# A fused transformer kernel: the masks of a top-16 attention move from VectorE to GpSimd for five of eight tiles

## The chip, the cores and the metric

One NeuronCore of one Trainium2 chip. The time is that of one execution on the device in microseconds (us); lower is better. Engines in the profile: PE is TensorE (PEld its weight loads), DVE is VectorE, ACT is ScalarE, POOL is GpSimd, SP is SyncE.

## The reference, cut to what matters

The program runs four blocks (L0 to L3) on x of shape (2, 1024, 256). The change is in the last, L3, between its cross-attention that keeps the 16 largest of 64 scores in each head, and its gated MLP:

```python
TOPK, H, D, HID = 16, 16, 16, 1024

def _topk_cross_attn(h, ctx, ...):
    q = (h @ w_q + b_q).reshape(B, L, H, D)
    kv = (ctx @ w_kv + b_kv).reshape(B, Lc, 2, H, D)       # Lc = 64
    scores = einsum('bqhd,bkhd->bhqk', q, k) / sqrt(D)
    top_s, top_i = jax.lax.top_k(scores, TOPK)
    attn = jax.nn.softmax(top_s, axis=-1)
    o = (attn weighted sum of the 16 rows of v that top_i names)
    return o @ w_co + b_co

def _swiglu(h, ...):
    u = h @ w_m1 + b_m1
    a, b = (u[..., :HID], u[..., HID:])
    return jax.nn.silu(a) * b @ w_m2 + b_m2

h = _ln(x) * (1 + sc_mca) + sh_mca
h = _topk_cross_attn(h, context, ...)
x = x + h * g_mca
h = _ln(x) * (1 + sc_mlp) + sh_mlp
x = x + _swiglu(h, ...) * g_mlp
```

## The kernel before, in words

Each engine has its own program, written out by hand; semaphores tie them together. A loop of two iterations runs over the batch (1024 tokens each), and inside it the blocks follow one another. The 1024 tokens of a batch are T = 8 tiles of 128 tokens (one token in each partition), and NB = 2 blocks of TB = 4 tiles. In the top-16 stage a tile is a matrix of 128 x 1024 scores: 16 heads of 64 context positions.

A tile t goes through these steps; the functions carry these names in the code:

- PE `top_scores(t)` (L1143) writes the scores to PSUM, ACT `top_copy(t)` (L1602) copies them into `prob3`, a ring of three buffers ("prob" in the profile).
- DVE `best(t)` (L2193) takes the 8 largest of each head into `m8` ("m" in the profile), 16 instructions MAX8, one for each head. DVE `mark(t)` (L2198) writes a copy of the scores into `taken`, where those 8 are replaced by LOWEST (16 pairs of MATCH_VALUE_LOAD and MATCH_REPLACE8). DVE `next_best(t)` (L2205) and `mark_next(t)` (L2210) do the same once more on `taken`. What equals LOWEST in `taken` then is the top 16. `taken` and `m8` have two buffers each.
- POOL `centre(t)` (L2405) subtracts each head's maximum from `prob3` as soon as `mark(t)` is done; ACT `exp(t)` (L1606) exponentiates it.
- DVE `mask(t)` (L2216) multiplies the exponentials by (taken == LOWEST), in one instruction, SCALAR_TENSOR_TENSOR.
- PE `top_turn(t)` (L1158) transposes the result, in two halves, ACT `turned(t)` (L1613) copies it into `probT`, PE `top_values(t)` (L1165) multiplies by the values and the ones that give the sums.
- DVE `divide(t)` (L1845, L1848) divides by the sums; PE `top_turn_outputs(t)` (L1172) turns the output, ACT `outputs3(t)` (L1617) copies it into `oT`.

Between these, PE runs matmuls on a constant tile (`keep_busy`, L565) that compute nothing which is used.

After four tiles the first block's output goes through the projection `wco` (PE L448), is turned (L589) and added to x on DVE (`add(0, 6)`: L1812 and the statistics L1795 to L1800); POOL's `ln(7, (0,))` (L2292) makes the reciprocal deviation, DVE `normalise(7, 0)` (L1805) the normalised tokens, PE turns them (L457), and ACT writes them twice (L1290): `hT` in full and `hs` rounded. The difference between the two, `hTlo`, is made by POOL's `tokens3_lo(0)` (L2410). Then the MLP of block 0 begins, while tiles 5 to 7 are still in the top-16 stage: PE `up(n)` (L1188), ACT `hidden(n)` (L1629 and L1290) reads it, POOL `times(n)` (L2416) multiplies the two halves, ACT `product_hi(n)` (L1640) rounds the product, POOL `product_lo(n)` (L2421) takes the rest, PE `down(n)` (L1217) uses both. For n < 5 the last three are POOL's, for later n they are DVE's.

Every engine works strictly in the order that is written, so a wait holds back all that stands behind it on that engine. The lines that set DVE's order are in the loop over t at the end of the stage; for POOL they are the plain list of calls behind `centre(0)`.

## Time and profile before

| | |
|---|---|
| three runs | 1786.18, 1791.75, 1791.81 us |
| median | 1791.75 us |
| the profiled execution: its own time | 1789.12 us |
| its span, first to last instruction | 1787.0 us |
| mean granted TensorE clock over the span | 0.951 |
| busy: PE, PEld | 1575.8 us (88%), 917.6 us |
| busy: DVE, ACT, POOL | 1082.2 us (61%), 812.6 us (45%), 417.7 us (23%) |
| the top-16 stage, first `best` to last `divide` | 750.46 to 867.90 us and 1604.48 to 1720.69 us |

The profile gives for each instruction its start and length on its engine, and, in square brackets, how long the engine sat idle before it and which instruction released it. The stage occurs twice, once for each batch, about 854 us apart. The granted clock is given as a share of full speed, where 1.00 is 2.4 GHz and 0.50 is 1.2 GHz.

### The profile page before, as it was taken

To read this page: it belongs to the slowest core of one execution; us is meant where nothing else is said; L and a number is where in the kernel's file an instruction comes from. 1 tells how busy PE (TensorE), PEld (TensorE's weight loads), DVE (VectorE), ACT (ScalarE), POOL (GpSimd) and SP (SyncE) were. 2 spreads that over 40 slices of the span, in tenths; PEclk is the share of its full clock that TensorE was granted. 3 is DMA by queue.
4 is the path that set the end of the run, shared out by engine and by line. 5 is a ranking of instruction groups with operands and counts; after the bars stand their busy time and mean duration, and the time that the engine had idled before them with its cause. 6 is when DMAs were issued, how large, how long until landed. Compare 5 with 4: busy or idle time off the path is not lost.

```text
span 1787.0 us, 27133 instructions
## 1 busy us (share of the span) xinstructions
PE 1575.8 (88%) x9541; PEld 917.6 (51%) x9541; DVE 1082.2 (61%) x2933; ACT 812.6 (45%) x1283; POOL 417.7 (23%) x418
## 2 busy tenths in 40 slices
PE   3789998999988989877878899899998888987888
PEld 1536564434343756455653556543443365654566
DVE  1464243899726338799536433479991643879963
ACT  1134331388843535324533434138886353442454
POOL 0140003433006024113205000153300602412230
PEclk8799999999999999999998999999999999999899
DMA  9200004422010000000050000352201000000004
GB/s 318 95 1 1 0 1 135 61 38 38 2 71 1 1 1 2 1 1 1 1 166 2 1 1 1 111 84 38 38 2 72 1 1 1 2 1 1 1 1 141
DMA packets 43332, 64.02 MB, mean 36 GB/s; under 512 B 8634, under 2 KB 32061, under 8 KB 42301
## 3 DMA queue, kind: packets, MB, share of 16 engines
q1 hardware_dynamic: 32845, 40.73, 6.9%
q0 software_dynamic: 8448, 14.96, 5.6%
q10 hardware_dynamic: 1904, 6.55, 0.9%
q8 instruction: 81, 1.33, 0.3%
q14 instruction: 54, 0.44, 0.1%
HBM read 47.28 MB, written 2.10 MB: 28 GB/s over the span
## 4 chain that ended last, share of the span: by engine, by line
PE 38%; issue 37%; POOL 12%; DVE 8%; ACT 3%; SPq 2%; DMA 1%; POOLq 0%; ACTq 0%; DVEq 0%
PE ps L932 7%; PE ps L944 7%; PE ps L1188 4%; PE ps L448 3%; POOL wkblk L2396 3%; PE ps L1022 3%; PE ps L917 3%; PE ps L1030 2%; PE ps L565 2%; PE ps L1217 2%; DVE taken L2198 2%; DVE taken L2210 1%; POOL rstd L2292 1%; DVE m L2193 1%; PE ps L457 1%
## 5 line engine op out<-in xcount | busy, mean ns | idle before, releaser
L2067 DVE TENSOR_REDUCE mm<-ps 128x1 f32<-128x1024 f32 x256 | 309.6, 1223 | 36.7 <-PE ps L917 30.0
L1490 ACT ACTIVATE pt<-ps 128x512 f32<-128x512 f32 x512 | 276.9, 598 | 62.8 <-PE ps L932 53.6
L2292 POOL TENSOR_TENSOR rstd<-ve,minus_half 128x4 f32<-128x4 f32 x32 | 36.2, 1130 | 810.7 <-DVE ve L1800 810.7
L932 PE MATMUL ps<-qx,kx 64*128 64x512 f32 x512 | 192.0, 452 | 1.8 <-ACT pt L1490 1.0
L917 PE MATMUL ps<-kx,qx 48*128 48x512 f32 x512 | 189.5, 450 | 1.7 <-DVE mm L2067 1.7
L944 PE MATMUL ps<-pt,v 128*32 128x256 f32 x2048 | 161.2, 396 | 0.0
L932 PEld LDWEIGHTS ps<-qx,kx 64*128 64x128 f32 x512 | 80.0, 186 | 98.2 <-ACT pt L1490 92.9
L1956 DVE TENSOR_TENSOR rlo<-ring,rhi 128x512 fp32r<-128x512 f32 x48 | 33.2, 692 | 127.7 <-ACT ring L1441 127.6
L917 PEld LDWEIGHTS ps<-kx,qx 48*128 48x128 f32 x512 | 76.6, 187 | 25.8 <-issue 15.4
L944 PEld LDWEIGHTS ps<-pt,v 128*32 128x32 f32 x2048 | 43.3, 109 | 87.8 <-ACT pt L1490 63.7
L457 PE MATMUL ps<-ident,xhat 128*128 128x128 f32 x288 | 45.0, 309 | 44.9 <-DVE xhat L1805 43.2
L565 PE MATMUL ps<-filler 128*128 128x512 f32 x258 | 81.8, 439 | 0.2
L2334 POOL DMA_DIRECT2D qx<-mxT x64 | 31.8, 506 | 211.2 <-ACT mxT L1482 190.8
L2396 POOL TENSOR_TENSOR wkblk<-kT,head_mask 128x1024 f32<-128x1024 f32 x32 | 60.5, 1896 | 85.3 <-PE ps L1085 82.2
L1812 DVE TENSOR_TENSOR x<-x,ps 128x1024 f32<-128x1024 f32 x32 | 39.0, 1218 | 67.6 <-PE ps L589 67.5
L1441 ACT ACTIVATE rhi<-ps,mod 128x512 fp32r<-128x512 f32 x48 | 33.1, 689 | 102.2 <-PE ps L722 102.2
L1290 ACT ACTIVATE hT<-ps,mod 128x512 f32<-128x512 f32 x48 | 35.1, 775 | 86.4 <-PE ps L457 86.4
L457 PEld LDWEIGHTS ps<-ident,xhat 128*128 128x128 f32 x288 | 38.1, 159 | 59.7 <-DVE xhat L1805 52.0
L1581 ACT ACTIVATE wprobT<-ps 128x1024 f32<-128x1024 f32 x32 | 32.8, 1023 | 75.1 <-PE ps L1097 75.1
L1859 DVE TENSOR_REDUCE mxw<-ps 128x16 f32<-128x1024 f32 x32 | 37.7, 1219 | 48.1 <-PE ps L606 48.1
L1085 PE MATMUL ps<-wkblk,qT 128*128 128x512 f32 x128 | 60.0, 594 | 1.5 <-DVE v L2140 1.5
L1805 DVE TENSOR_SCALAR xhat<-x,mv,rstd 128x256 f32<-128x256 f32 x128 | 46.3, 424 | 21.4 <-POOL rstd L2292 20.9
(322 smaller groups left out, 3454.0 us busy)
## 6 DMA issues: line engine op xcount, KB each, us to landing
w<-in_L_xcond_e_w_dram SPq DMA_DIRECT2D x9, 512.0 KB, 8.0
w<-in_L_xcond_e_w_dram SPq DMA_DIRECT2D x3, 1536.0 KB, 12.1
wm<-in_L_xcond_W_mlp_dram SPq DMA_DIRECT2D x4, 1024.0 KB, 7.9
qx<-q_hi POOLq DMA_DIRECT2D x64, 64.0 KB, 2.6
kx<-k_hi POOLq DMA_DIRECT2D x64, 64.0 KB, 2.8
w3a<-in_L_xcond_w_m_dram SPq DMA_DIRECT2D x2, 2048.0 KB, 8.1
s_ada<-in_L_xcond_w_ada_dram ACTq DMA_DIRECT2D x1, 2304.0 KB, 14.7
qx<-q_lo POOLq DMA_DIRECT2D x32, 64.0 KB, 2.6
```

The costliest lines, as they stand in the source:

```text
L448: ins = pe.matmul(ps[:, bank, :], w[:, c, m * P:(m + 1) * P], src[:, c, :], start=c == 0, stop=c == KC - 1)
L457: ins = pe.transpose(ps[:, bank + c, t * P:(t + 1) * P], src[:, TB * k + t, c * P:(c + 1) * P], ident[:, :])
L565: pe.matmul(ps[:, bank, :], filler[:, 0:P], filler[:, :], start=True, stop=True)
L917: ins = pe.matmul(ps[:, bank + half, :], qx[r, p % 4, t * P:(t + 1) * P], kx[r, p % 4, half * 512:(half + 1) * 512], start=True, stop=True)
L932: pe.matmul(ps[:, bank, :], kx[r, p % 4, kc * P:(kc + 1) * P], qx[r, p % 4, half * 512:(half + 1) * 512], start=True, stop=True).then_inc( ...
L944: ins = pe.matmul(ps[o:o + 32, 7, q:q + BLK // 2], v2[:, kc, VS * (2 * p + e):VS * (2 * p + e) + 32], pt[:, (2 * kc + e) % 8, half * BLK + ...
L1085: ins = pe.matmul(ps[:, 2 * (u % 2) + half, :], qT[:, t // TB, c, t % TB * P:(t % TB + 1) * P], wkblk[:, u % 2, 4 * half:4 * half + 4, :]. ...
L1188: ins = pe.matmul(ps[:, 4 + i, :], w3ap[wp][:, c, (NC_HID * i + m) * P:(NC_HID * i + m + 1) * P], src[:, c, :], start=(wp, part, c) == (0, ...
L1490: act.activation(pt[:, u % 8, half * 512:(half + 1) * 512], ps[:, bank, :], ACT.Exp, scale=QK_SCALE).then_inc(st_read, 1)
L2067: return dve.tensor_reduce(mm[:, p % 2, e, t:t + 1], place(), X, ALU.max).then_inc(ring_read, 1)
L2292: pool.tensor_tensor(rstd[:, k, :], ve[:, k, :], minus_half[:, :], ALU.pow).then_inc(rstd_ready, 1)
L2396: pool.tensor_tensor(wkblk[:, u % 2, :, :], kT3[:, t // TB, c, t % TB * P:(t % TB + 1) * P].unsqueeze(1).broadcast_to([P, HC, P]), head_ma ...
```

## The change

- A constant `N_PMASK = 5`. For tiles 0 to 4 the mask is no longer DVE's. POOL's new `mask(t)` waits for `mark_next(t)` (semaphore `top_taken`), turns `taken` in place into ones and zeros (TENSOR_SCALAR is_equal, 128x1024), and, once `exp(t)` is done, multiplies `prob3` by it (TENSOR_TENSOR, 128x1024). Tiles 5 to 7 keep DVE's mask.
- `top_ready` becomes two semaphores, one for each engine that masks; PE's `top_turn(t)` waits for the one of its tile. DVE's `best(t)` for t = 2 to 6 waits in addition until POOL has masked tile t - 2, whose buffers it will overwrite.
- DVE's `divide(t - 1)` comes behind `mark_next(t)` for t = 1, 2 and 3 (before: ahead of it) and between `next_best(t)` and `mark_next(t)` for t = 4 to 7. `add(0, 6)` of tile 5 comes behind `mark(5)`, `normalise(7, 0)` behind `next_best(5)` and ahead of the division.
- `tokens3_lo(0)` is DVE's, behind `mark_next(5)` and ahead of `mask(5)`; before, it was POOL's.
- POOL's `centre(5)` comes ahead of `ln(7, (0,))`, and `centre(6)` ahead of `product_lo(0)` and `times(1)`.
- ACT's `product_hi(0)` comes ahead of `hidden(1)`.
- `keep_busy` between the tiles 0 to 3 has 3 and 8 matmuls where it had 4 and 10.

```diff
--- before.py
+++ after.py
@@ -81,6 +81,7 @@
 N_CU = NB * KC
 N_POOL3 = 5
 N_DVE3 = NB * NC_HID - N_POOL3
+N_PMASK = 5


 def key_entries(p):
@@ -291,8 +292,8 @@
...
-        ts_ready, ts_read, top_marked, top_sub, top_exp, top_ready, tp_turned, tpT_ready, tpv_done, to_ready, to_turned, toT_ready = (sem(n) for n in (
...
+        ts_ready, ts_read, top_marked, top_sub, top_exp, tp_turned, tpT_ready, tpv_done, to_ready, to_turned, toT_ready = (sem(n) for n in (
...
@@ -308,6 +309,7 @@
         h2_done, h2_ready, w22_done = sem("h2_done"), sem("h2_ready"), sem("w22_done")
         h3_done, h3_read, w32_done = sem("h3_done"), sem("h3_read"), sem("w32_done")
         w3_hi, w3_split, hs3_hi, hs3_lo, h3_hi = sem("w3_hi"), sem("w3_split"), sem("hs3_hi"), [sem("hs3_lo0"), sem("hs3_lo1")], sem("h3_hi")
+        top_taken, top_flag, top_ready = sem("top_taken"), sem("top_flag"), [sem("top_ready_pool"), sem("top_ready_dve")]
         prod_pool, prod_dve, lo_pool, lo_dve = sem("prod_pool"), sem("prod_dve"), sem("lo_pool"), sem("lo_dve")
         v_done, v_ready, v2_clear = sem("v_done"), sem("v_ready"), sem("v2_clear")
         ring_ready, ring_read, hi_ready, lo_ready, full_done, full_ready = (sem(n) for n in (
@@ -1146,7 +1148,10 @@

                 def top_turn(t):

-                    pe.wait_ge(top_ready, t0 + t + 1)
+                    if t < N_PMASK:
+                        pe.wait_ge(top_ready[0], b * N_PMASK + t + 1)
+                    else:
+                        pe.wait_ge(top_ready[1], b * (T - N_PMASK) + t + 1 - N_PMASK)
                     if t == 0:
                         pe.wait_ge(qT_ready, b * 2 * N_Q + 6)
                     else:
@@ -1227,10 +1232,10 @@
                 top_scores(1)
                 for t in range(TB):
                     top_scores(t + 2)
-                    keep_busy(5, 4)
+                    keep_busy(5, 3)
                     if t:
                         top_turn_outputs(t - 1)
-                    keep_busy(5, 10)
+                    keep_busy(5, 8)
                     top_turn(t)
                     top_values(t)
                 keep_busy(5, 4)
@@ -1668,8 +1673,8 @@
                 ln(7, 0, (mod, M3_SC_ML, M3_SH_ML), 6)
                 hidden(0)
                 turned(5)
+                product_hi(0)
                 hidden(1)
-                product_hi(0)
                 exp(6)
                 product_hi(1)
                 hidden(2)
@@ -2188,6 +2193,8 @@

                 def best(t):
                     dve.wait_ge(ts_read, t0 + t + 1)
+                    if 2 <= t < N_PMASK + 2:
+                        dve.wait_ge(top_ready[0], b * N_PMASK + t - 1)
                     dve.sem_inc(passed, 1)
                     for h in range(H):
                         ins = dve.max(m8[:, t % 2, h, 0:8], scores_by_head(t)[:, h, :])
@@ -2208,12 +2215,15 @@
                 def mark_next(t):
                     for h in range(H):
                         ins = dve.match_replace(taken_by_head(t)[:, h, :], m8[:, t % 2, h, 8:16], taken_by_head(t)[:, h, :], LOWEST)
-                    link(ins)
+                    if t < N_PMASK:
+                        ins.then_inc(top_taken, 1)
+                    else:
+                        link(ins)

                 def mask(t):

                     dve.wait_ge(top_exp, t0 + t + 1)
-                    dve.scalar_tensor_tensor(prob3[:, t % 3, :], taken[:, t % 2, :], LOWEST, prob3[:, t % 3, :], ALU.is_equal, ALU.mult).then_inc(top_ready, 1)
+                    dve.scalar_tensor_tensor(prob3[:, t % 3, :], taken[:, t % 2, :], LOWEST, prob3[:, t % 3, :], ALU.is_equal, ALU.mult).then_inc(top_ready[1], 1)

                 def divide(t):
                     outputs(t, 3, t0, tpv_done, to_turned, to_ready)
@@ -2244,18 +2254,21 @@

                 for t in range(T):
                     best(t)
+                    mark(t)
                     if t == TB + 1:
                         add(0, 6)
-                    mark(t)
-                    if t in (TB, TB + 1):
+                    next_best(t)
+                    if t == TB + 1:
+                        normalise(7, 0)
+                    if t >= TB:
+                        divide(t - 1)
+                    mark_next(t)
+                    if 1 <= t < TB:
                         divide(t - 1)
                     if t == TB + 1:
-                        normalise(7, 0)
-                    next_best(t)
-                    if t and t not in (TB, TB + 1):
-                        divide(t - 1)
-                    mark_next(t)
-                    mask(t)
+                        tokens3_lo(0)
+                    if t >= N_PMASK:
+                        mask(t)
                 divide(7)
                 times(5)
                 add(1, 2)
@@ -2404,10 +2417,14 @@
                     sc = prob3[:, t % 3, :].rearrange("p (h s) -> p h s", s=S)
                     pool.tensor_tensor(sc, sc, m8[:, t % 2, :, 0].unsqueeze(2).broadcast_to([P, H, S]), ALU.subtract).then_inc(top_sub, 1)

-                def tokens3_lo(k):
-
-                    pool.wait_ge(hs3_hi, b * NB + k + 1)
-                    pool.tensor_tensor(hTlo[:, k, :, :], hT[:, k, :, :], hs3[k][:, :, :].bitcast(F32), ALU.subtract).then_inc(hs3_lo[k], 1)
+                def mask(t):
+
+                    pool.wait_ge(top_taken, b * N_PMASK + t + 1)
+                    pool.sem_inc(passed, 1)
+                    pool.tensor_scalar(taken[:, t % 2, :], taken[:, t % 2, :], LOWEST, None, ALU.is_equal).then_inc(top_flag, 1)
+                    pool.wait_ge(top_flag, b * N_PMASK + t + 1)
+                    pool.wait_ge(top_exp, t0 + t + 1)
+                    pool.tensor_tensor(prob3[:, t % 3, :], prob3[:, t % 3, :], taken[:, t % 2, :], ALU.mult).then_inc(top_ready[0], 1)
                 n0 = b * NB * NC_HID

                 def times(n):
@@ -2424,15 +2441,16 @@
                 pool.wait_ge(v3_ready, b * NB + NB)
                 pool.sem_inc(passed, 1)
                 split3(2, w3b_hi[1][:, :, :], w3b_lo[:, NC_HID // 2:, :], w3b[:, NC_HID // 2:, :])
-                for t in range(1, 5):
+                mask(0)
+                for t in range(1, N_PMASK):
                     centre(t)
+                    mask(t)
+                centre(5)
                 ln(7, (0,))
-                centre(5)
-                tokens3_lo(0)
                 times(0)
+                centre(6)
                 product_lo(0)
                 times(1)
-                centre(6)
                 product_lo(1)
                 times(2)
                 product_lo(2)
```

How the order of the instructions moves. First DVE, the whole of tile 2, with the start of tile 3. In the rows m_151 is `m8` and prob_211 is `prob3`. Before:

```order
L2193 MAX m_151<-prob_211 128x8 x16
L2198 MATCH_REPLACE taken<-m_151,prob_211 128x64 x16
L2205 MAX m_151<-taken 128x8 x16
L1845 RECIPROCAL rs<-ps 128x16
L1848 TENSOR_TENSOR o_tok<-ps,rs 128x256
L2210 MATCH_REPLACE taken<-m_151,taken 128x64 x16
L2216 SCALAR_TENSOR_TENSOR prob_211<-taken,prob_211 128x1024
L2193 MAX m_151<-prob_211 128x8 x16
```

Now:

```order
L2200 MAX m_151<-prob_211 128x8 x16
L2205 MATCH_REPLACE taken<-m_151,prob_211 128x64 x16
L2212 MAX m_151<-taken 128x8 x16
L2217 MATCH_REPLACE taken<-m_151,taken 128x64 x16
L1850 RECIPROCAL rs<-ps 128x16
L1853 TENSOR_TENSOR o_tok<-ps,rs 128x256
L2197 REGISTER_ALU
L2200 MAX m_151<-prob_211 128x8 x16
```

The wide masking instruction is gone from the tile, and the division stands last in it. Second, DVE in tile 5, from `mark(5)` to the start of tile 6. Before:

```order
L2198 MATCH_REPLACE taken<-m_151,prob_211 128x64 x16
L1845 RECIPROCAL rs<-ps 128x16
L1848 TENSOR_TENSOR o_tok<-ps,rs 128x256
L1805 TENSOR_SCALAR xhat<-x,mv,rstd 128x256 x4
L2205 MAX m_151<-taken 128x8 x16
L2210 MATCH_REPLACE taken<-m_151,taken 128x64 x16
L2216 SCALAR_TENSOR_TENSOR prob_211<-taken,prob_211 128x1024
L2193 MAX m_151<-prob_211 128x8 x16
```

Now:

```order
L2212 MAX m_151<-taken 128x8 x16
L1810 TENSOR_SCALAR xhat<-x,mv,rstd 128x256 x4
L1850 RECIPROCAL rs<-ps 128x16
L1853 TENSOR_TENSOR o_tok<-ps,rs 128x256
L2217 MATCH_REPLACE taken<-m_151,taken 128x64 x16
L2237 TENSOR_TENSOR hTlo<-hT,hs_0_204 128x1024
L2226 SCALAR_TENSOR_TENSOR prob_211<-taken,prob_211 128x1024
L2197 REGISTER_ALU
L2200 MAX m_151<-prob_211 128x8 x16
```

`tokens3_lo(0)` (the write of hTlo) now stands on DVE between the search of tile 5 and its mask. Third, POOL from tile 4's centring to the MLP's second product. Before:

```order
L2405 TENSOR_TENSOR prob_211<-prob_211,m_151 128x1024
L2291 REGISTER_ALU
L2292 TENSOR_TENSOR rstd<-ve,minus_half 128x4
L2403 REGISTER_ALU
L2405 TENSOR_TENSOR prob_211<-prob_211,m_151 128x1024
L2410 TENSOR_TENSOR hTlo<-hT,hs_0_204 128x1024
L2416 TENSOR_TENSOR gate_0_195<-gate_0_195,up_0_197 128x512
L2421 TENSOR_TENSOR prod_lo_206<-gate_0_195,prod_hi_208 128x512
L2416 TENSOR_TENSOR gate_0_195<-gate_0_195,up_0_197 128x512
L2403 REGISTER_ALU
L2405 TENSOR_TENSOR prob_211<-prob_211,m_151 128x1024
```

Now:

```order
L2418 TENSOR_TENSOR prob_211<-prob_211,m_151 128x1024
L2422 REGISTER_ALU
L2424 TENSOR_SCALAR taken<-taken 128x1024
L2427 TENSOR_TENSOR prob_211<-prob_211,taken 128x1024
L2416 REGISTER_ALU
L2418 TENSOR_TENSOR prob_211<-prob_211,m_151 128x1024
L2304 REGISTER_ALU
L2305 TENSOR_TENSOR rstd<-ve,minus_half 128x4
L2433 TENSOR_TENSOR gate_0_195<-gate_0_195,up_0_197 128x512
L2416 REGISTER_ALU
L2418 TENSOR_TENSOR prob_211<-prob_211,m_151 128x1024
L2438 TENSOR_TENSOR prod_lo_206<-gate_0_195,prod_hi_208 128x512
```

POOL has two instructions more in each of the tiles 0 to 4, no hTlo, and centres tile 6 after one product instead of three instructions later.

## Rows read from the trace of the kernel before

**Rows 1.** The page's head and part 1: busy time and share of the span.
```profile
span 1787.0 us, 27133 instructions
PE 1575.8 (88%) x9541; PEld 917.6 (51%) x9541; DVE 1082.2 (61%) x2933; ACT 812.6 (45%) x1283; POOL 417.7 (23%) x418
```
**Rows 2.** The chain that ended last, 744 to 890 us: shares by line.
```profile
by line: issue 13.8%; DVE taken L2198 10.9%; DVE taken L2210 8.5%; PE ps L1188 7.3%; DVE m L2193 7.2%; PE ps L448 6.6%; DVE m L2205 5.7%; POOL gate L2416 5.1%; PE ps L1143 3.9%; POOL prob L2405 2.6%; POOL prod_lo L2421 2.6%; POOL hTlo L2410
```
**Rows 3.** Timeline, DVE, tile 1 of the first batch: start, length, line, operation.
```profile
763.49 2.12 DVE L2193 MAX8 m<-prob 128x8 f32<-128x64 f32 x16
...
771.15 0.26 DVE L1845 RECIPROCAL rs<-ps 128x16 f32<-128x16 f32 x1
...
775.01 1.22 DVE L2216 SCALAR_TENSOR_TENSOR prob<-taken,prob 128x1024 f32<-128x1024 f32 x1
776.15 2.12 DVE L2193 MAX8 m<-prob 128x8 f32<-128x64 f32 x16
```
**Rows 4.** Timeline, DVE, the mask of tile 0.
```profile
762.35 1.23 DVE L2216 SCALAR_TENSOR_TENSOR prob<-taken,prob 128x1024 f32<-128x1024 f32 x1 [1.01 <-ACT prob L1606]
```
**Rows 5.** Timeline, ACT and PE: exponential, transposes, values of tile 1.
```profile
772.68 1.05 ACT L1606 ACTIVATE prob<-prob 128x1024 f32<-128x1024 f32 x1
776.29 1.09 PE L1158 MATMUL ps<-ident,prob 128*128 128x128 f32 x8 [1.64 <-DVE prob L2216]
778.12 2.00 PE L1165 MATMUL ps<-vx,probT 128*128 128x64 f32 x16 [0.74 <-ACT probT L1613]
```
**Rows 6.** Groups of POOL by form: line, operation, count, busy us, mean ns, idle before.
```profile
L2405 POOL TENSOR_TENSOR prob<-prob,m 128x1024 f32<-128x1024 f32 x16 | 30.9, 1933 | 101.9 <-DVE taken L2198 101.9
...
L2372 POOL TENSOR_TENSOR w3b_lo<-w3b,w3b_hi 128x1024 fp32r<-128x1024 f32 x4 | 9.5, 2364 | 0.3
...
L2370 POOL CAST w3b_hi<-w3b 128x1024 fp32r<-128x1024 f32 x4 | 4.2, 1044 | 0.0
```
**Rows 7.** Timeline, DVE, from tile 5 on, first and then second batch.
```profile
814.11 2.12 DVE L2193 MAX8 m<-prob 128x8 f32<-128x64 f32 x16
...
823.41 2.35 DVE L1805 TENSOR_SCALAR xhat<-x,mv,rstd 128x256 f32<-128x256 f32 x4
...
831.07 1.23 DVE L2216 SCALAR_TENSOR_TENSOR prob<-taken,prob 128x1024 f32<-128x1024 f32 x1
832.21 0.98 DVE L2193 MAX8 m<-prob 128x8 f32<-128x64 f32 x7
...
847.79 2.12 DVE L2193 MAX8 m<-prob 128x8 f32<-128x64 f32 x16
...
882.17 1.38 DVE L1805 TENSOR_SCALAR xhat<-x,mv,rstd 128x256 f32<-128x256 f32 x4 [0.30 <-POOL rstd L2292]
...
1679.33 2.35 DVE L1805 TENSOR_SCALAR xhat<-x,mv,rstd 128x256 f32<-128x256 f32 x4
...
1689.12 2.11 DVE L2193 MAX8 m<-prob 128x8 f32<-128x64 f32 x16
...
1701.78 2.12 DVE L2193 MAX8 m<-prob 128x8 f32<-128x64 f32 x16
```
**Rows 8.** Timeline, ACT and POOL: rounded tokens hs, and hTlo, both batches.
```profile
1684.21 1.45 ACT L1290 ACTIVATE hs<-ps,mod 128x512 fp32r<-128x512 f32 x2
...
831.22 3.31 POOL L2410 TENSOR_TENSOR hTlo<-hT,hs 128x1024 fp32r<-128x1024 f32 x1 [6.57 <-ACT hs L1290]
...
1685.73 2.39 POOL L2410 TENSOR_TENSOR hTlo<-hT,hs 128x1024 fp32r<-128x1024 f32 x1 [5.17 <-ACT hs L1290]
```
**Rows 9.** Timeline, PE: transposes of tile 7, both batches.
```profile
862.76 1.07 PE L1158 MATMUL ps<-ident,prob 128*128 128x128 f32 x8 [0.43 <-ACT oT L1617]
...
1715.78 1.04 PE L1158 MATMUL ps<-ident,prob 128*128 128x128 f32 x8
```
**Rows 10.** Stretches of 4 us: length, busy PE, PEld, DVE, ACT, POOL, granted clock.
```profile
824.00:828.00 4.00, 4.00 (x15) 3.28 (x15) 3.96 (x22) 1.44 (x2) 0.65 (x1) 0.58 0.00 0
...
1662.00:1666.00 4.00, 3.53 (x8) 1.79 (x7) 3.96 (x38) 1.33 (x2) 0.83 (x1) 0.50 0.00 0
```

2 lines of the change are left out of this document (1 added, 1 removed).

## The prediction

> **What bounds the kernel now.** The page's head gives the frame [rows 1]: the profiled execution has a span of 1787.0 us and a time of 1789.12, against a median of 1791.75 of the three runs. PE is busy for 88% of the span and DVE for 61%, but these are means over stages with different limits, so I read the stage of the change by itself. In the chain of waits between 744 and 890 us [rows 2] the four parts of DVE's search (L2193, L2198, L2205, L2210) hold 32.3% (7.2, 10.9, 5.7 and 8.5), more than any other engine's lines. The timeline of tile 1 shows the loop that sets the pace [rows 3]: DVE starts tile 1 at 763.49 and tile 2 at 776.15, 12.66 us apart, with no idle time in between. PE, on the other hand, waits 1.64 us there for the mask [rows 5]. So until the MLP begins, the stage lasts as long as DVE's list, and a microsecond taken from that list is one off the time, so long as what takes its place is ready in time.
>
> **What the change takes from DVE, tiles 0 to 4.** From the start of the mask at 775.01 to the next tile at 776.15 are 1.14 us, and about 0.03 of hand-over ahead of it go too: 1.17 us a tile, a new period of 11.49 [rows 3]. Five tiles give 5.85. The mask of tile 0 also waited 1.01 us for the exponential [rows 4], a wait that is now POOL's: 6.86.
>
> **What it gives POOL, and whether DVE must wait for it.** Let M be the end of `mark_next(t)`. POOL needs the flags (F) and the product.
> - The product: a multiplication of two whole 128x1024 operands. `centre`, whose second operand is one number for each head, takes 1.93 us; the subtraction of two whole operands takes 2.36 [rows 6]. The product resembles the second, so I take 2.36.
> - The flags: the trace has no TENSOR_SCALAR with is_equal on POOL. It has one input, like the CAST of 128x1024 in 1.04, which is the nearest row and the lower end; the two-input instruction, 2.36, is the upper end of what I hold likely [rows 6]. I take 1.1.
> - The product also waits for `exp(t)`. That stands on ACT behind `outputs3(t - 1)`, so it follows the division: in tile 1 DVE ended its division where it began `mark_next`, 771.15 + 0.64 = 771.79, and the exponential ended at 772.68 + 1.05 = 773.73, 1.94 later [rows 3, 5]. Now the division ends at M + 0.64, so the exponential ends at M + 2.58, and any F up to about 2.4 is hidden behind it: both my ends cost the same.
> - The product therefore ends near M + 5.05. From the start of the transposes to the end of the values are 778.12 + 2.00 - 776.29 = 3.83 us [rows 5]: M + 8.93. DVE asks for them at `divide(t)`, one period later, at M + 11.49. That leaves 2.56 us. Tiles 0 to 2 make DVE wait for nothing.
> - Tile 3 is another matter, since `divide(3)` stands ahead of `mark_next(4)`. DVE gets there 7.66 us after it began tile 4 (771.15 - 763.49 in rows 3), at M + 8.30, and waits 0.63. For the same reason all that hangs on it (the output projection of block 0) comes early.
>
> A row that might speak against it: does POOL's work slow the search? `centre` runs beside MAX8 in most of its 16 tiles, and its mean is 1933 ns [rows 6], while DVE's 16 MAX8 take 2.11 or 2.12 in every row shown. I give this nothing. The shorter `keep_busy` (3 and 8 instead of 4 and 10) frees time on PE only, which waits anyway.
>
> DVE thus starts tile 5 by 6.86 - 0.63 = 6.2 us earlier, at 807.9 instead of 814.11 [rows 7].
>
> **Tile 5: half of it is given back.** Before, DVE took 832.21 - 814.11 = 18.10 us for it [rows 7]. Two things leave the search part: the mask (1.14, counted apart below), and a delay of `normalise(7, 0)`: 2.35 us in both batches, against 1.38 where POOL has nothing beside it, and `centre(5)`, which it met, is now done before it (-0.97) [rows 7]. So DVE is through `mark_next(5)` at 807.9 + 15.99 = 823.9, and had ended its division 3.22 before that, at 820.7. Now `tokens3_lo(0)` needs `hs`. From the end of the division to `hs` it took 1685.73 - 1679.33 = 6.40 us in the second batch and 831.22 - 823.41 = 7.81 in the first, over the turned outputs, the fillers, the transposes and ACT [rows 7, 8]. So `hs` is there at 827.1, and DVE stands idle for 3.2 us, with the mask of tile 5 and the whole search of tile 6 queued behind. This is the new wait of the change. Then hTlo (1.22, by the two-input instruction of the same size in rows 3, against 2.39 to 3.31 on POOL [rows 8]) and the mask (1.14): tile 6 starts at 829.5. Before, it was 832.21 in the first batch and 1689.12 in the second, which is 835.1 with the 854.0 between the batches taken off.
>
> Here page and trace can be weighed. The row: hTlo took 3.31 us on POOL in the first batch and 2.39 in the second, and in the first a DVE mask of 1.23 us had begun 0.15 us earlier [rows 7, 8]. The Trainium skill, "SBUF — State Buffer", section "Who interferes with whom", says that a DVE instruction with two SBUF inputs and a GpSimd instruction that reads SBUF exclude each other, the later one standing still until the first is done; the trace agrees, 0.92 us of excess. By it the new order is safe in tiles 0 to 4, since beside POOL's product stand only MAX8 and MATCH_REPLACE8, with one input each.
>
> **Tiles 6 and 7, and what hangs on them.** With a mask of its own and nothing late, a tile takes 12.66: tile 7 starts at 842.2, against 847.79 (-5.6), and in the second batch at 1696.2 against 1701.78 (-5.6) [rows 7]. Everything on POOL and ACT is earlier by as much or more: `up(0)` no longer waits for hTlo from POOL, `product_hi(0)` does not wait behind `hidden(1)`, and `centre(6)` is ahead of the products, so the exponential of tile 6 is done before its mask is due. PE began the transposes of tile 7 14.97 us after DVE began that tile in the first batch and 14.00 in the second [rows 7, 9]. With 14.00 they stand at 856.2 against 862.76 (-6.6) and 1710.2 against 1715.78 (-5.6). From there on nothing is changed; PE, ACT and DVE run the same list, earlier.
>
> **The sum.** 6.6 + 5.6 = 12.2 us. I take off 1.4, the difference between 7.81 and 6.40, for one passage of the hs chain at the lower clock: the first batch had a granted clock of 0.58 at 824 to 828 (1.00 is 2.4 GHz, 0.50 is 1.2 GHz) after PE had stood waiting for DVE's outputs [rows 10], and something of that kind will meet one batch again. That makes 10.8 us: 1778.3 for an execution like the profiled one, and **1781.0 us** against the median, 0.6% less. Below 0.3% (5.4 us) a measurement of this kernel can't tell a change from none, as the three runs themselves lie 5.6 apart.
>
> **Rivals.**
> 1. *The clock takes half of it.* In the second batch the granted clock was 0.50 from 1662 to 1666 [rows 10], the lower of its two levels, and the projection, the scores and the turning of block 0 stood in it. With 11 fillers a tile instead of 14, PE has one longer wait before each mask. At half speed transposes and values take 3.09 us more, M + 12.0, so each `divide` of tiles 0 to 2 waits 0.5 and `divide(3)` 3.7: up to 5 us in a batch; and a stretch that falls into the MLP costs PE, which sets the pace there, half of its length. For it: such stretches occurred in both batches. Against: PE's busy share of a period stays what it was, since the period shrinks along with the fillers. It leaves a gain of 2 to 8 us: 1784 to 1790, 1787 as its middle.
> 2. *POOL's flag instruction is dear (the slower side).* One mechanism: values end at M + F + 0.2 + 6.2, and DVE waits from F = 5.1 on; at F = 6.2 the wait of 1.17 has eaten a tile's gain. At F = 7 each of three divisions waits 1.9 and `divide(3)` 5.1, some 11 in a batch against the 5 to 6 gained: 1791.75 + 2 x 6 = 1804 us. For it: no row shows the operation, and on POOL a form of instruction can cost far more per element than another. Against: all forms of 1024 elements on POOL lie between 1.04 and 2.36 [rows 6]. The Trainium skill, "GPSIMD Engine Reference", section "Instruction dispatch", states about 6 us for the first call of a freshly loaded kernel of GpSimd's software, with no visible instruction; were that paid whenever TENSOR_SCALAR comes between other forms, it would be this case. Each CAST between subtractions shows 1.04 with no such gap [rows 6], so I hold it unlikely.
> 3. *The new wait in tile 5 is longer.* If `hs` comes at 7.8 instead of 6.4 in both batches and the exponential or the products then make tile 6 late by some 2 us, 7 us remain: 1785.
> 4. *The change doesn't do what it says*, because `exp` or POOL's order (mask ahead of the next centring) ties the loop to 12.66 again: 1791. With 2.56 us of slack in each tile, unlikely.
>
> **How the numbers follow.** The forecast has 0.58 (gains of 8 to 14), with its own range of 1777 to 1784. Rival 1 has 0.18, rival 3 0.13, rival 4 0.04, rival 2 0.07. The predicted time is that of the forecast. Leaving out 2 in 10 (rival 2, and the far ends of the others), the range is 1776 to 1789, which takes in the gain without any deduction and a profile that stands to its median as this one does. Faster by over 0.3% (below 1786.4): the forecast, rival 3 and a third of rival 1, 0.77. Within 0.3%: the rest of rival 1 and rival 4, 0.16. Slower: 0.07.
>
> **What would show it.** On DVE a period of 11.5 us in tiles 1 to 3, no idle time before `divide(0)` to `divide(2)`, and about 0.6 before `divide(3)`; POOL's flags near 1.1 us and its product near 2.4, the latter released by `exp`. An idle stretch of about 3 us on DVE before hTlo. `best(6)` some 2.7 us earlier than before in the first batch, the transposes of tile 7 5.6 to 6.6. I am wrong if the flags take over 5 us, if DVE waits before its divisions, or if the stage ends early and the MLP behind it, at a lower clock, gives the time back.

## The result and the profile after

The kernel with the change takes 1801.08 us (median of 5 runs, 1800.44 to 1802.99), the kernel before 1791.3 (median of 5, the three of the table above among them): a ratio of 1.0067 with an interval of 1.0049 to 1.0085. It is **slower** by some 10 us, where I had forecast 11 us less. The prediction was wrong, in sign and outside its range.

| profiled execution | before | after |
|---|---|---|
| span | 1787.0 us | 1798.8 us |
| first `best` to `best(7)`, batch 1 | 97.33 us | 103.86 us |
| the same, batch 2 | 97.30 us | 103.96 us |
| mean granted clock | 0.951 | 0.939 |

The stage between the start of tile 0 and the start of tile 7 is 6.5 and 6.7 us longer, together more than the 11.8 by which the span grew. So the loss is in the stage. This is the head of the page after, which answers to [rows 1]:

```profile
span 1798.8 us, 27129 instructions
PE 1590.6 (88%) x9517; PEld 928.7 (52%) x9517; DVE 1071.6 (60%) x2925; ACT 813.9 (45%) x1283; POOL 460.6 (26%) x436
```

DVE lost 10.6 us of work, as planned, and POOL gained 43. PE is busy for 15 us more although it has 24 matmuls less: it runs at a lower clock.

The times between the starts of one `best` and the next, a tile's period, in batch 1 (batch 2 is within 0.1 us after, and before but for tile 5, 20.81 there, tile 6, 12.66, and tile 4, 12.85):

| tile | 0 | 1 | 2 | 3 | 4 | 5 | 6 |
|---|---|---|---|---|---|---|---|
| before | 13.03 | 12.66 | 12.65 | 12.66 | 12.65 | 18.10 | 15.58 |
| forecast | 10.85 | 11.49 | 11.49 | 11.49 | 12.12 | 21.6 | 12.7 |
| after | 10.77 | 12.66 | 13.87 | 13.89 | 16.93 | 22.86 | 12.88 |

(The forecast row is the prediction's own working: 13.03 less 1.17 and 1.01 for tile 0, and the wait of 0.63 in tile 4.) Only tiles 0 and 6 came out near the forecast. DVE's timeline around the first two divisions, in answer to [rows 3]:

```profile
772.38 0.26 DVE L1850 RECIPROCAL rs<-ps 128x16 f32<-128x16 f32 x1 [1.16 <-PE ps L1170]
772.68 0.42 DVE L1853 TENSOR_TENSOR o_tok<-ps,rs 128x256 f32<-128x256 f32 x1
773.02 2.12 DVE L2200 MAX8 m<-prob 128x8 f32<-128x64 f32 x16
...
786.26 0.26 DVE L1850 RECIPROCAL rs<-ps 128x16 f32<-128x16 f32 x1 [2.38 <-PE ps L1170]
```

DVE now waits for PE's values before each division: 1.16, 2.38, 2.39 and, for `divide(3)`, 5.58. The forecast had none, none, none and 0.63. What PE did meanwhile, in answer to [rows 5]:

```profile
766.01 1.97 PE L1163 MATMUL ps<-ident,prob 128*128 128x128 f32 x8 [4.16 <-POOL prob L2427]
768.67 3.68 PE L1170 MATMUL ps<-vx,probT 128*128 128x64 f32 x16 [0.69 <-ACT probT L1618]
772.14 3.73 PE L1145 MATMUL ps<-kblk,qT 128*128 128x512 f32 x4
774.88 1.79 PE L567 MATMUL ps<-filler 128*128 128x512 f32 x3
776.50 0.38 PE L1177 MATMUL ps<-ident,o_tok 128*128 128x128 f32 x2
776.64 2.10 PE L567 MATMUL ps<-filler 128*128 128x512 f32 x8
780.82 1.09 PE L1163 MATMUL ps<-ident,prob 128*128 128x128 f32 x8 [2.07 <-POOL prob L2427]
782.65 3.57 PE L1170 MATMUL ps<-vx,probT 128*128 128x64 f32 x16 [0.74 <-ACT probT L1618]
786.01 3.73 PE L1145 MATMUL ps<-kblk,qT 128*128 128x512 f32 x4
788.75 1.69 PE L567 MATMUL ps<-filler 128*128 128x512 f32 x3
790.28 0.38 PE L1177 MATMUL ps<-ident,o_tok 128*128 128x128 f32 x2
```

Two things are to be seen. First, PE waited 4.16 us for POOL's first mask, and what followed ran at half speed: the values of tile 0 took 3.68 us, where those of tile 1 had taken 2.00 before [rows 5], and the scores 3.73, where they had taken 1.94 in the trace of the kernel before. Second, the division ended at 773.02 (where `best` begins), but its output was turned only at 776.50, 3.5 us later, because the scores of tile 3 and three fillers stand ahead of it. ACT and POOL show what hangs on that:

```profile
776.92 0.39 ACT L1622 ACTIVATE oT<-ps 128x256 f32<-128x256 f32 x1 [8.31 <-PE ps L1177]
777.21 1.05 ACT L1611 ACTIVATE prob<-prob 128x1024 f32<-128x1024 f32 x1
```

```profile
760.73 2.80 POOL L2424 TENSOR_SCALAR taken<-taken 128x1024 f32<-128x1024 f32 x1 [0.32 <-DVE taken L2217]
763.62 2.35 POOL L2427 TENSOR_TENSOR prob<-prob,taken 128x1024 f32<-128x1024 f32 x1
765.92 1.94 POOL L2418 TENSOR_TENSOR prob<-prob,m 128x1024 f32<-128x1024 f32 x1
771.42 2.77 POOL L2424 TENSOR_SCALAR taken<-taken 128x1024 f32<-128x1024 f32 x1 [3.56 <-DVE taken L2217]
778.41 2.35 POOL L2427 TENSOR_TENSOR prob<-prob,taken 128x1024 f32<-128x1024 f32 x1 [4.22 <-ACT prob L1611]
```

POOL had its flags for tile 1 at 774.19, and then stood 4.22 us for the exponential, which stands behind `outputs3(0)` on ACT. This is a **closed ring**: `divide(0)`, outputs turned, `outputs3(0)`, `exp(1)`, the product, the transposes, the values, `divide(1)`. Its parts add up: 772.38 to 776.50 (4.12 us, for the division and the rest of scores and fillers), to the exponential's end at 778.26 (1.76), to the product's end at 780.76 (2.50), to the values' end at 786.22 (5.46), and the next division begins at 786.26. That is the 13.88 us from one division to the next, and no longer DVE's list. The first and the last of these parts hold scores, fillers and values that ran at the lower clock.

The groups of POOL by form give the two prices that [rows 6] had only bounded:

```profile
L2424 POOL TENSOR_SCALAR taken<-taken 128x1024 f32<-128x1024 f32 x10 | 27.7, 2773 | 29.1 <-DVE taken L2217 29.1
L2427 POOL TENSOR_TENSOR prob<-prob,taken 128x1024 f32<-128x1024 f32 x10 | 23.5, 2350 | 30.2 <-ACT prob L1611 29.8
```

The product costs 2.35, as taken (2.36); the flags cost 2.77, above my upper end. Of POOL's idle time ahead of the product nearly all, 29.8 of 30.2 us, is a wait for the exponential.

The stretches of 4 us show the clock (the number before the last two of each row). After:

```profile
764.00:768.00 4.00, 1.97 (x8) 1.56 (x8) 3.84 (x33) 0.60 (x1) 3.86 (x2) 0.71 0.01 2
768.00:772.00 4.00, 3.33 (x16) 3.33 (x16) 3.20 (x32) 0.60 (x1) 0.58 (x1) 0.50 0.00 0
772.00:776.00 4.00, 4.00 (x7) 1.93 (x7) 3.55 (x27) 0.00 (x0) 2.19 (x1) 0.51 0.00 0
776.00:780.00 4.00, 2.74 (x13) 1.86 (x11) 3.85 (x37) 2.25 (x3) 1.59 (x1) 1.00 0.00 0
780.00:784.00 4.00, 2.45 (x15) 2.21 (x16) 3.84 (x38) 1.09 (x2) 2.65 (x2) 0.85 0.03 6
784.00:788.00 4.00, 4.00 (x14) 2.97 (x14) 1.71 (x11) 0.00 (x0) 2.77 (x1) 0.50 0.00 0
```

It is at the lower level (0.50, 1.2 GHz) once in each tile. Before, the same 24 us had a granted clock of 1.00 throughout, and only 788 to 800 was lower (0.81, 0.50, 0.84).

Last, tile 5 on DVE, in answer to [rows 7] and [rows 8]:

```profile
824.80 1.22 DVE L1817 TENSOR_TENSOR x<-x,ps 128x1024 f32<-128x1024 f32 x1 [1.73 <-PE ps L591]
...
830.14 1.38 DVE L1810 TENSOR_SCALAR xhat<-x,mv,rstd 128x256 f32<-128x256 f32 x4
...
838.29 1.23 DVE L2237 TENSOR_TENSOR hTlo<-hT,hs 128x1024 fp32r<-128x1024 f32 x1 [3.04 <-ACT hs L1295]
```

The wait for `hs`, 3.04 us, and the shorter `normalise(7, 0)`, 1.38, are as forecast (3.2 and 1.38). A wait of 1.73 for the turned residual is new in this batch; before, batch 2 alone had one, of 1.75. Tile 7 began at 853.45, and PE began its transposes at 867.45, the 14.00 us later that I had taken, but after instead of before the 862.76 of [rows 9].

### The profile page after: what moved, and what is told of

Same layout as the page of the kernel before. It is cut to its first block, busy times and chain, and to the rows that moved or that the text cites. A ratio compares the mean times of both kernels' runs of the same rounds, so it can differ in the third digit from the quotient of the medians.

```text
span 1798.8 us, 27129 instructions
## 1 busy us (share of the span) xinstructions
PE 1590.6 (88%) x9517; PEld 928.7 (52%) x9517; DVE 1071.6 (60%) x2925; ACT 813.9 (45%) x1283; POOL 460.6 (26%) x436
## 4 chain that ended last, share of the span: by engine, by line
PE 40%; issue 36%; POOL 11%; DVE 6%; ACT 3%; SPq 2%; DMA 1%; POOLq 0%; ACTq 0%; DVEq 0%
PE ps L934 7%; PE ps L946 7%; PE ps L1193 4%; POOL wkblk L2409 3%; PE ps L450 3%; PE ps L1024 3%; PE ps L919 3%; PE ps L1032 2%; PE ps L567 2%; PE ps L1170 2%; PE ps L1222 2%; PE ps L1145 2%; POOL rstd L2305 1%; DVE taken L2205 1%; POOL prob L2427 1%
## 5 line engine op out<-in xcount | busy, mean ns | idle before, releaser
L1024 PE MATMUL ps<-hs,w1s 128*128 128x512 f32 x192 | 52.6, 418 | 5.8 <-ACT hs L1295 5.8
```

The costliest lines, as they stand in the source:

```text
L1024: ins = pe.matmul(ps[:, m % 4, :], w1s[:, wp, c, m * P:(m + 1) * P], hs[:, k, sp, c, :], start=(wp, sp, c) == (0, 0, 0), stop=(sp, c) == ( ...
```

## The experiments

Two things could cause the loss, and the runs separate them. **Theory A, the order:** the late division ties the exponential of tile t (behind `outputs3(t - 1)` on ACT) into the ring above. **Theory B, the clock:** POOL's first mask is late, PE waits 4.16 us, the clock falls, and with the fewer fillers it falls again in every tile. Further suspects were the masks on POOL as such, the fillers and the new order in tile 5. All ratios are against the kernel before, measured beside each run on the same chip. The runs come from three chips, so ratios are compared, and a median only with the one beside it.

### Fillers: hold the clock, or put the old number back

The kernel of the change, with more matmuls that hold the clock:

```diff
-                    keep_busy(5, 8)
+                    keep_busy(5, 14 if t else 24)
```

> The changed kernel with more constant matmuls in PE's wait for the mask: 24 instead of 8 ahead of tile 0's transposes, 14 instead of 8 ahead of those of tiles 1 to 3. Nothing else differs. Theory clock: the changed kernel loses because the granted clock falls to 0.50 once in every tile, from the 4.16 us wait before the first mask on; at full clock the values are ready before DVE asks. Then the clock stays near 1.00 here, DVE's period falls from 13.87 to about 11.5 us, its wait before divide(3) from 5.6 to 1 or 2 us, and the time to 1779 to 1784. Theory latency: the two POOL instructions and the exponential ahead of them make the loop long at any clock. Then the period stays over 13 us and the time is 1800 or more, since the added matmuls can only delay PE.

Measured: 1791.61 us, ratio 1.0016 (0.9982 to 1.0050). The periods of batch 1 were 10.78, 11.40, 11.39, 13.07, 15.74, 22.58 and 12.87. For three tiles the stage ran at the forecast pace. PE was at full clock up to 784, and the order of the change did no harm there: in tile 1 `mark_next` ended at 776.98, and the exponential, still behind `outputs3(0)`, at 779.78, which is 2.8 us later:

```profile
778.73 1.05 ACT L1611 ACTIVATE prob<-prob 128x1024 f32<-128x1024 f32 x1
```

Then the clock fell, and the ring was back:

```profile
784.00:788.00 4.00, 3.62 (x17) 3.35 (x18) 3.97 (x39) 0.33 (x1) 0.97 (x1) 0.63 0.01 2
788.00:792.00 4.00, 4.00 (x8) 1.91 (x7) 3.93 (x32) 0.00 (x0) 2.77 (x1) 0.52 0.00 0
```

```profile
801.43 0.26 DVE L1850 RECIPROCAL rs<-ps 128x16 f32<-128x16 f32 x1 [1.59 <-PE ps L1170]
```

So the longer row of fillers takes away most of the loss, and the median shows no gain; the clock fell in spite of it. In batch 2 the stage up to `best(7)` took 94.51 us, 2.8 less than before, in batch 1 97.83, 0.5 more. The profiled span is 3.1 us longer than before, but tile 0 began 5.0 us later, in a part that no edit touches; from tile 0 on it is 1.9 us shorter. The same kernel with the old number of fillers:

```diff
-                    keep_busy(5, 3)
+                    keep_busy(5, 4)
...
-                    keep_busy(5, 8)
+                    keep_busy(5, 10)
```

> The changed kernel with keep_busy of 4 and 10 as before the change, instead of 3 and 8. Theory clock, in the form that the fewer fillers did it: clock near the level of before, time near 1782. Theory clock, in the form that POOL's later first mask (4.16 us of PE waiting, now 3.4) did it: the clock still falls, time 1797 to 1802. Theory latency: 1801.

Measured: 1800.32 us, 1.0051 (1.0026 to 1.0075), with periods of 10.79, 12.64, 14.19, 13.92, 16.96, 22.62 and 12.89, as in the change. Three fillers a tile more do nothing; the fewer fillers are not what lowered the clock in the changed kernel. The other way round, the kernel before with the new, smaller numbers:

```diff
-                    keep_busy(5, 4)
+                    keep_busy(5, 3)
...
-                    keep_busy(5, 10)
+                    keep_busy(5, 8)
```

> The kernel before with keep_busy of 3 and 8 instead of 4 and 10, no other edit. If the fewer fillers alone bring the clock down: PE waits some 2.1 us for each mask instead of 1.6, the clock falls more often than once in the stage, time 1792 to 1800. If they don't: 1788 to 1792, as before.

Measured: 1787.77 us, 0.9981 (0.9954 to 1.0008). One tile took 13.76 with a wait of 1.14 for the exponential, and tile 5 of batch 1 took 20.63, but tile 6 12.66, together 33.3 as before (33.7). Here the fewer fillers did cost clock: 0.50 from 776 to 784, where it had been 1.00, and a mean of 0.945 instead of 0.951. DVE's list sets the pace there, and hides most of what PE loses. And the kernel before with more fillers, which came last, as the control for the first experiment:

```diff
-                    keep_busy(5, 10)
+                    keep_busy(5, 15)
```

> The kernel before with keep_busy of 4 and 15 instead of 4 and 10: the clock held, and nothing else of the change. It prices what the clock alone is worth to the kernel before. There DVE sets the pace at 12.66 us whatever the clock, so no more than 1.75 us (the wait for the turned residual in the second batch) can be won in a batch: 1786 to 1791. If it comes near 1781, the gain of the version with both edits is the fillers' and not the order's.

Measured: 1788.42 us, 0.9998 (0.9987 to 1.0009), a mean granted clock of 0.955 instead of 0.951, and the same time from `best(0)` to `best(7)` (97.37 and 97.35 us); in the stretch from 764 to 804 the clock was 1.00, where it had been 0.91. Holding the clock is worth nothing where DVE sets the pace. It is worth something in the changed kernel, whose ring goes through PE.

### The order: is it POOL's masks, or the late division?

The kernel of the change with all masks back on DVE, everything else left as changed:

```diff
-N_PMASK = 5
+N_PMASK = 0
...
-                mask(0)
-                for t in range(1, N_PMASK):
+                for t in range(1, 6):
                     centre(t)
-                    mask(t)
-                centre(5)
```

> The changed kernel with all masks back on DVE (N_PMASK = 0); the moved divisions, hTlo on DVE, centre(6) first and the fillers of 3 and 8 stay. Theory clock and theory latency alike put the loss on the masks: period 12.7 us, time 1785 to 1792. If the division behind mark_next or hTlo on DVE is what costs, the time stays near 1800.

Measured: 1808.43 us, 1.0092 (1.0065 to 1.0119). My expectation was wrong: without POOL's masks the kernel is slower still. Its periods are 13.03, 14.90, 14.64, 14.88, 12.65, 22.77 and 12.87, and DVE's timeline says why:

```profile
773.13 0.26 DVE L1850 RECIPROCAL rs<-ps 128x16 f32<-128x16 f32 x1
773.42 0.42 DVE L1853 TENSOR_TENSOR o_tok<-ps,rs 128x256 f32<-128x256 f32 x1
775.99 1.23 DVE L2226 SCALAR_TENSOR_TENSOR prob<-taken,prob 128x1024 f32<-128x1024 f32 x1 [2.14 <-ACT prob L1611]
```

The division doesn't wait; the mask does, for the exponential, which ended 2.1 us after the division. PE reached the turning of the outputs early here and waited for DVE, so the step from division to exponential is the short one that I knew from [rows 3] and [rows 5]. Now that the division stands last, those 2.1 us lie open. So the order costs by itself here, without POOL's masks and with the values at full clock (2.00 us).

The opposite: POOL's masks stay, and the divisions go back ahead of `mark_next` in tiles 1 to 3:

```diff
-                    if t >= TB:
+                    if t:
                         divide(t - 1)
                     mark_next(t)
-                    if 1 <= t < TB:
-                        divide(t - 1)
```

> The changed kernel with the division back ahead of mark_next in tiles 1 to 3; masks stay on POOL. Theory order: the exponential comes early again, the product starts when the flags end (2.9 us after mark_next), but DVE now asks for the values 8.3 us after mark_next, while they take 5.3 + 3.9 = 9.2 at full clock (wait 0.9, period 12.4, just below the 12.66 of before) and 11.6 at half clock (wait 3.3, period 14.8). Time 1788 to 1810 according to the clock; the clock decides here.

Measured: 1807.41 us, 1.0102 (1.0069 to 1.0135). The divisions wait 4.46, 3.53, 4.35 and 3.52 us for the values, with periods of 14.9 to 15.8. POOL's masks are available too late for the old place. This holds for the clock of this run (a mean of 0.67 from 764 to 804); the case at full clock, with the period of 12.4 that I expected, wasn't run. What was tried next leaves the division where the change put it and moves the exponential.

### The exponential ahead of the outputs

```diff
                 for t in range(1, TB):
+                    exp(t)
                     outputs3(t - 1)
-                    exp(t)
                     top_copy(t + 2)
```

> The changed kernel with one edit on ACT: in tiles 1 to 3 exp(t) stands ahead of outputs3(t - 1). Theory order: in the changed kernel the division behind mark_next delays outputs3, and the exponential with it; so divide(t - 1), outputs turned, outputs3, exp(t), product, transposes, values, divide(t) form a closed ring of 13.87 us. With the exponential first, the product can start when the flags end, 2.9 us after mark_next instead of 7.2, and even at half clock the values are ready some 11.6 us after mark_next: a period of 11.5 to 12, the wait before divide(3) 1 to 3.5 us, time 1780 to 1786. Theory clock alone: the first wait for POOL's mask (4.2 us) is still there, the clock still falls, period over 13, time 1797 or more.

Measured: 1784.65 us against 1787.66, 0.9978 (0.9958 to 0.9998). The periods are 10.78, 12.64, 11.39, 11.77, 13.48, 22.49 and 12.85. The start is the same as in the change, the long wait for the first mask and the half clock included; but the ring is gone. Tile 1 on POOL:

```profile
771.88 2.77 POOL L2424 TENSOR_SCALAR taken<-taken 128x1024 f32<-128x1024 f32 x1 [3.57 <-DVE taken L2217]
774.73 2.38 POOL L2427 TENSOR_TENSOR prob<-prob,taken 128x1024 f32<-128x1024 f32 x1
```

The product follows the flags at once. By itself this one line, moved, turns +0.7% into -0.2%. So the slow clock alone doesn't make the loss, which is against theory B alone; and the first run, with more fillers, showed two tiles at full clock in which the order alone didn't make it either. Each edit by itself takes away about as much: up to `best(7)` the order gives 95.40 and 95.48 us in the two batches, the fillers 97.83 and 94.51, where the change had 103.86 and 103.96, and the intervals of the two ratios overlap. The loss takes both, the order that ties the exponential to PE and a PE at half clock. Here the clock still falls (a mean of 0.74 from 764 to 804), tile 1 still takes 12.64, and `divide(3)` waits 2.10 us. Both edits together, the exponential first and the longer row of fillers:

```diff
+                    exp(t)
                     outputs3(t - 1)
-                    exp(t)
...
-                    keep_busy(5, 8)
+                    keep_busy(5, 14 if t else 24)
```

> As the last, with the fillers of the run that held the clock (3, and 24 for tile 0 or 14). Order and clock together: period 11.4 in tiles 1 to 3, clock near 1.00 up to tile 4, time 1778 to 1784. If order is all, no faster than the last run within 2 us; if the added fillers delay the masks' transposes, slower than it.

Measured: 1780.84 us, 0.9967 (0.9939 to 0.9996). The periods are 10.78, 11.41, 11.39, 11.40, 12.64, 21.29 and 12.84, tile 7 starts 91.75 and 91.71 us after tile 0, and the clock has a mean of 0.91 from 764 to 804. The forecast's own periods add up to 91.7. DVE's timeline at the first three divisions and at `divide(3)`:

```profile
776.58 0.25 DVE L1850 RECIPROCAL rs<-ps 128x16 f32<-128x16 f32 x1
...
787.97 0.25 DVE L1850 RECIPROCAL rs<-ps 128x16 f32<-128x16 f32 x1
...
799.37 0.25 DVE L1850 RECIPROCAL rs<-ps 128x16 f32<-128x16 f32 x1
...
808.89 0.26 DVE L1850 RECIPROCAL rs<-ps 128x16 f32<-128x16 f32 x1 [1.27 <-PE ps L1170]
```

Neither edit alone gives this pace. The fillers don't keep the clock up throughout; it fell here as it did with the fillers alone:

```profile
784.00:788.00 4.00, 4.00 (x18) 3.48 (x19) 3.96 (x40) 1.06 (x1) 0.56 (x1) 0.58 0.01 2
788.00:792.00 4.00, 4.00 (x10) 2.16 (x9) 3.93 (x33) 0.00 (x0) 3.67 (x2) 0.57 0.00 0
```

These two kernels differ only in the place of `exp`. After about the same fall from 784 to 792, tile 3 took 13.07 us there and 11.40 here. This pair shows best what the order does: it decides how much of a slow stretch of PE reaches DVE.

### Tile 5 and the place of hTlo

What do the edits of tile 5 cost by themselves? The masks go to DVE (POOL's list as in the other run with them there) and the divisions ahead of `mark_next`:

```diff
-N_PMASK = 5
+N_PMASK = 0
...
-                    if t >= TB:
+                    if t:
                         divide(t - 1)
                     mark_next(t)
-                    if 1 <= t < TB:
-                        divide(t - 1)
```

What is left of the change is `tokens3_lo(0)` on DVE, the order in tile 5, the earlier `centre` and `product_hi(0)`, and the fillers:

> The changed kernel with all masks on DVE and the division ahead of mark_next: what is left of the change is hTlo on DVE, the orders in tile 5, centre(6) first, product_hi(0) first, fillers 3 and 8. Theory order: with masks on DVE, the division behind mark_next made the mask wait 2 us for the exponential in each of tiles 1 to 3 (period 14.9); ahead of it the period is 12.7 again, and the time 1784 to 1793. If hTlo on DVE (idle 4.5 us for hs) costs more than it gives, this run is above the kernel before by a few us.

Measured: 1792.76 us, 1.0031 (1.0010 to 1.0052). Tiles 5 and 6 together take 21.71 + 12.85 = 34.56 and 22.83 + 12.87 = 35.70 us, against 33.68 and 33.47 before. The tail loses 0.9 and 2.2 us. In batch 1 tile 2 also took 13.95, as one tile did in the kernel before with the same short row of fillers, so the stage as a whole lost 2.2 and 2.0. The new wait of the tail is the one for `hs`, 3.02 us in batch 1 and 4.61 in batch 2:

```profile
832.69 1.23 DVE L2237 TENSOR_TENSOR hTlo<-hT,hs 128x1024 fp32r<-128x1024 f32 x1 [3.02 <-ACT hs L1295]
```

So I moved it, on top of the two edits that worked. Once back to POOL, behind `ln(7, (0,))`:

```diff
                 ln(7, (0,))
+                tokens3_lo(0)
                 times(0)
...
-                    if t == TB + 1:
-                        tokens3_lo(0)
```

> The version with the exponential first and the clock held, with hTlo of block 0 back on POOL, behind ln(7, (0,)). There DVE waited 3.05 us for hs before hTlo, with the mask of tile 5 and all of tile 6 behind it. Theory: that wait and the 1.2 us of hTlo were on DVE's path; tile 5 falls from 21.3 to about 17.2 us, part of which is lost where DVE then waits for the values of tile 5, PE's up(0) ends some 1.2 us later. 1 to 4 us faster in each batch, time 1773 to 1779. Rival: in this part the path runs through up, POOL's products and down, not DVE; then time 1780 to 1784, the same or a little slower.

Measured: 1777.46 us, 0.9936 (0.9913 to 0.9958); tiles 5 and 6 take 17.16 + 16.29 us instead of 21.29 + 12.84. And once on DVE, but behind `best(6)`, so that a piece of search lies over the wait:

```diff
                     best(t)
+                    if t == TB + 2:
+                        tokens3_lo(0)
                     mark(t)
...
-                    if t == TB + 1:
-                        tokens3_lo(0)
```

> The same version, with hTlo still DVE's, but behind mask(5) and best(6) instead of ahead of them, so that it stands where hs has just arrived. Theory: the 3.05 us of idle time on DVE are filled with 3.3 us of mask and search; hTlo is not later than before by more than 0.3 us, tile 6's search ends 3 us earlier, and the transposes of tile 5 are not held up: up to 3 us faster in each batch, 1775 to 1780. Rival (the path is in the MLP's products): no change, 1780 to 1782.

Measured: **1774.86 us**, 0.9930 (0.9907 to 0.9953), the lowest ratio of all, and clearly faster than the kernel before. The subtraction starts without any wait:

```profile
824.72 2.12 DVE L2200 MAX8 m<-prob 128x8 f32<-128x64 f32 x16
826.87 1.23 DVE L2237 TENSOR_TENSOR hTlo<-hT,hs 128x1024 fp32r<-128x1024 f32 x1
...
835.44 0.26 DVE L1850 RECIPROCAL rs<-ps 128x16 f32<-128x16 f32 x1 [1.96 <-PE ps L1170]
```

The intervals of the last two overlap, so which place is the better one stays open. Both show that the wait in tile 5 was a matter of the place in the list: tile 5 falls from 21.29 to 17.15, and 2.9 of these 4.1 us are given back in tile 6, where `divide(5)` then waits 1.96 for the values. The transposes of tile 7 begin 104.45 and 105.97 us after tile 0, instead of 106.81 and 106.67 in the kernel with the two edits alone, and 112.30 and 111.30 before. So 2.4 and 0.7 us are left there. What this is worth at the end is not clear: from tile 0 on, the profiled execution is 1.3 us shorter than that with the two edits alone (5.1 us with `hTlo` on POOL), the other 5.0 us of its lead being an earlier tile 0, and the ratios' intervals (0.9907 to 0.9953, 0.9939 to 0.9996) overlap by a little.

## Why the prediction was wrong

**The bound** (DVE's list sets the pace) was right for the kernel before; more fillers or fewer changed nothing clear of noise there. It stopped being true with the change, since the new ring, at half clock, was longer than the shortened list.

**What DVE loses, 1.17 us a tile**: right. Tile 0 took 10.77, and wherever nothing waited a tile took 11.38 to 11.43 (forecast 11.49).

**"The exponential ends at M + 2.58"**: this is the step that failed. I had the 1.94 us from the end of the division to the end of the exponential from tile 1 of the kernel before, and carried it over as if it belonged to the chain itself. It was so short only because PE had the scores and the fillers behind it and stood idle in front of the turning of the outputs. This is that row of the kernel before, tile 1:

```profile
771.92 0.44 PE L1172 MATMUL ps<-ident,o_tok 128*128 128x128 f32 x2 [1.78 <-DVE o_tok L1848]
```

When the division has to wait for the values, PE comes straight from them, and the scores and the fillers are still ahead of the turning, here at half clock. In tile 1 `mark_next` ended at 771.2 and the exponential at 778.26: M + 7.0. From the end of the division it was 5.2 us instead of 1.94. The product ended at 780.76, M + 9.5 instead of M + 5.05, and from the transposes to the end of the values it took 5.4 us instead of 3.83; so the slack of 2.56 us became a wait of 2.38. The delay after the division is no constant of the order: with PE at full clock (the run with 24 and 14 fillers, tile 1) the exponential ended at M + 2.8, close to the forecast, and nobody waited. What the sum lacked is that this path leads through PE, and that it grows with the values at a slow clock. The new order's own consequence for ACT's list, with the exponential behind an instruction that waits for the division, I had seen and written down; I had not asked where PE stands at that moment. (Where the mask is DVE's, the late division costs some 2 us a tile, 2.14, 1.89 and 2.14, even with PE in time.)

**The flags, 1.1 us**: mis-sized. They take 2.77, above the upper end of 2.36, so both of my neighbouring rows were too cheap. (That all forms of 1024 elements lie between 1.04 and 2.36 wasn't right either: [rows 8] has hTlo at 2.39 and 3.31.) In tiles 1 to 3 this was covered by the wait for the exponential. In tile 0, where `exp(0)` is early, nothing covered it: PE waited 4.16 us for the first mask, where it had waited 0.21 before. I priced tile 0 on DVE only, and named nobody who waits for the mask on PE. With flags of 1.1 us this wait would have been some 2.5 (an estimate, 4.16 less 2.80 and plus 1.1); whether the clock would have fallen then wasn't tested.

**Rival 1, the clock**: its mechanism came true, its size didn't. I had it take half of a gain and gave it 0.18. It priced the half clock for the transposes and the values only (3.09 us), and not for the scores and fillers ahead of the outputs, through which the exponential comes late. After the wait of 4.16 us the granted clock was 0.50 once in every tile, and waits like that of 2.07 us before the transposes of tile 1 came again in each. That the closed ring is what made them come again is not shown: with the exponential moved the clock fell too (a mean of 0.74 from 764 to 804, and 0.70 in the change). The argument against it, that PE's busy share of a period stays what it was, left out that one wait becomes longer. It is one half of the cause and not the whole: with the exponential moved, the kernel was faster at a mean granted clock of 0.938, as low as that of the change.

**Rival 2, the dear flags** had the sign right and the mechanism wrong. With a price of 2.77 us its own formula gives no wait (it begins at 5.1), and the kernels with the same flags and the exponential first are faster than before. The 6 us for a first call, which the Trainium skill, "GPSIMD Engine Reference", section "Instruction dispatch", states, appear in no row: POOL was idle for 0.32 us before the first flags, and in that time the trace has two MODIFY_POOL_CONFIG of 11 ns; the flags took 2.80, and the product followed at 763.62, 0.09 later.

**SBUF contention**: by the row in the prediction and by the Trainium skill, "SBUF — State Buffer", section "Who interferes with whom", POOL's product beside the search should cost nothing. The trace agrees: beside the product of 778.41 the 16 MAX8 of 778.52 took 2.13 us, against 2.11 to 2.13 before.

**Tile 5**: the wait for `hs` was 3.04 us (forecast 3.2). The tile took 22.86 instead of 21.6, mainly since `add(0, 6)` waited 1.73 for the residual of block 0, whose chain hung on the late `divide(3)` and a slow PE. That this edit gives more than it takes was not so: by itself the tail lost 0.9 and 2.2 us, as measured with the masks back on DVE.

**Tiles 6 and 7**: 12.88 for 12.7, and 14.00 for 14.00, both right, but starting from the wrong point.

**The sum**: 12.2 us of gain in the stage were forecast, 5.6 in each batch up to tile 7 and one more in the first. The kernel with the exponential first and more fillers gains 97.33 - 91.75 = 5.6 and 97.30 - 91.71 = 5.6 there (5.5 and 4.6 at the transposes of tile 7), and is 6.8 us faster in its median, 1780.84 beside 1787.66. So the terms on DVE were priced about rightly, and the forecast describes a kernel with a different order on ACT and more fillers. That it fits to 0.1 us is luck: tile 4 took 12.64 for 12.12, tile 5 21.29 for 21.6. Of the 11.2 us in the two stages not all reach the end: the distance between the two batches' tiles 0 shrank by 3.6 and the rest behind the second by 4.5. That is 8.1; its profiled span is only 3.5 shorter, since tile 0 of batch 1 began at 755.01 instead of 750.46, in a part that no edit touches. This start lay anywhere from 746.8 to 755.4 over the kernels here. Where the 3.1 us between stage and end went wasn't tested.

## What to carry to other kernels

A duration between two events on different engines, read from one trace, holds only while the engine in the middle is ready when the first event comes (here 1.94 us before and 5.2 after). When an instruction is moved to the end of a list, ask for every engine downstream what stands ahead of its answer there, and which in-order list then carries the delay back: here one `exp` behind one `outputs3` closed a ring through four engines, harmless at full clock and 1.2 us a tile longer than before where the clock fell. If a ring closes, PE's clock is a part of it, and here one long wait was followed by a slow stretch in every tile after it; extra matmuls are worth something in a ring, and nothing beside a list that is longer. And a new wait in a list is cheapest behind a piece of work that doesn't depend on it: moving one subtraction behind `best(6)` took a wait of 3.05 us away, but only 2.4 us in one batch and 0.7 in the other were left at the last tile, since DVE then met the next wait.
